# A four-layer graph network kernel: sums merged into the convolutions, a reordered setup, split loads, and a head pass with stacked columns

## Chip, cores and metric

One core of a Trainium2 chip runs the whole kernel. The metric is device time in microseconds (us) of one execution, as the median of several. An engine is one of PE (TensorE), DVE (VectorE), ACT (ScalarE), POOL (GpSimd) and SP (SyncE, which here only issues DMAs).

## What is computed

`x` has 10000 rows of 768 values. Four graph layers follow each other, each ending in a layer norm of `x + layer(x)`. The edge list has 2500 random edges and one loop for each row.

```python
edge_index = jnp.stack([src, dst])
x = _layernorm(x + _L0_gnn_ref(x, edge_index, ...))      # 2 attention convolutions, then [x, out2] @ Wu + bu
x = _layernorm(x + _L1_gnn_ref(x, W_fc, attn_l, attn_r, W_res, src, dst))   # 12 heads of 64
x = _layernorm(x + _L2_gnn_ref(x, edge_index, W, b))     # one graph convolution
x = _layernorm(x + _L3_gnn_ref(x, W1, b1, W2, b2, edge_index))              # two graph convolutions

# a head of L1:            relu(h @ W_res.T + sum over its edges e of alpha_e * (h[src_e] @ W_fc.T))
# a convolution (L2, L3):  h = x @ W;  out = segment_sum(h[src] * dinv[src] * dinv[dst], dst) + b
```

## The kernel before, in words

The 10000 rows are cut into NT = 79 tiles of 128 rows (the last has 16). Every pass goes over the 79 tiles with `over_tiles`: four tiles written out, then a hardware loop of four tiles a turn, then the rest. Each engine has its own program, and semaphores order them. UNROLL = 4 is also the number of row buffers of a pass. KC = 6 is the number of 128-wide slices of 768. In time the kernel is a row of blocks; at the end of each every engine waits for the others and the block's semaphores are cleared.

- `first_layers` (0 to 1280 us). A setup folds the norm's factor and the two attention vectors into the first weight: PE transposes W1 (L1217), makes the bias columns `c_col` with 48 one-column products (L1223), and then `fold(s)` for six slices (L1236). ACT and DVE take the folded slices out (L1115, L1109, L682, L671). ACT's queue issues the small loads first, among them 16 one-column loads of the attention vectors (L1100). `fold_const` on PE (L1246, L1250) makes a constant row from `c_col`; on PE it stands after the transposes of tile 0 and before those of tile 1, on DVE after the low part of tile 0 (L712). Then come 158 tiles of products (L1279).
- `update_pass` (1284 to 1595 us). A tile loads a row block of `out2` (L1474, into `o2`) and of `u` (L1477, into `ut`), both on one semaphore for each slot; PE turns `o2` (L1575), ACT copies it, PE multiplies (L1585), DVE adds `ut` (L1489) and takes the statistics, ACT takes the root (L1533) and normalises (L1541). `y` has two buffers. POOL clears `rows_x` (15860 columns, L1461) for the next block, and after it the padding of `o2` (L1462, L1464), for which PE waits.
- `third_layer` (1596 to 1745 us) makes the attention sums of the edges.
- `heads_pass` (1749 to 2097 us). SP loads two 64x64 weights, each twice into the diagonal blocks of a 128x128 tile (L2204, transposed element by element), then the rows (L2211). POOL fetches the summed row of the edges by an indirect DMA (L2226) and scales the own row by head (`hds_x`, L2235), DVE adds the fetched row (L2264). PE turns six slices of the row (L2355) and six of `hds_x` (L2358), ACT copies all twelve (L2312), and PE makes six pairs of 128-column products (L2368, L2369). DVE adds and takes the statistics, ACT normalises.
- Three times: `multi_sum`, a block of some 40 us, and `conv_pass`, a block of some 560 us. `multi_sum` loads and splits the next weights, fetches S2 = 6 chunks of 128 rows with indirect DMAs (L2066) into `rows`, which DVE has cleared (L2097), sums them by destination on PE (L2143, L2149), and stores the sums with indirect DMAs (L2070). `conv_pass` clears `more` on POOL (L2431), fetches one row for each row of the tile (L2440), builds `x` (L2512, L2452), turns it (L2570), splits it into a high and a low part (L2518, L2460) and makes 36 products a tile (L2581).

Of the kernel before, what the change touches and what calls it, by code (L numbers as in the profile page):

```python
# [5 lines left out]
F32 = mybir.dt.float32  # L6
# [6 lines left out]
P = 128  # L13
N = 10000
# [75 lines left out]
def over_tiles(eng, step, drain=0):  # L90


    for t in range(UNROLL):
        step(t, t, 0)
    with eng.Fori(1, NT // UNROLL) as i:
        for j in range(UNROLL):
            step(i * UNROLL + j, j, i)
    for t in range(NT // UNROLL * UNROLL, NT + drain):
        step(t, t % UNROLL, t // UNROLL)


def back(t, slot, turn, lag):

    return t - lag, (slot - lag) % UNROLL, turn + (slot - lag) // UNROLL
# [31 lines left out]
def build(nc, a, out):  # L136
# [15 lines left out]
    with ExitStack() as ctx:  # L152
# [32 lines left out]
        multi_sum(nc, g, "l2", x2, a["L2_gnn_W"], a["L2_gnn_b"])  # L185
        conv_pass(nc, g, "cv", x2, x3[0:N, :], res=x2)
        multi_sum(nc, g, "l3a", x3, a["L3_gnn_W1"], a["L3_gnn_b1"])
        conv_pass(nc, g, "c3a", x3, x2[0:N, :])
        multi_sum(nc, g, "l3b", x2, a["L3_gnn_W2"], a["L3_gnn_b2"])
        conv_pass(nc, g, "c3b", x2, out, res=x3, last=True)  # L190


# [22 lines left out]
def first_layers(nc, g, a, packed, packed2, sources, agg, h1, sc1, h2, out2, u, x2, x3):  # L215
# [3 lines left out]
    with ExitStack() as ctx:  # L219
# [85 lines left out]
        b_col, g_col, b1_col, c_col = sb("b_col", [P, KC]), sb("g_col", [P, KC]), sb("b1_col", [96, 8]), sb("c_col", [96, 8])  # L305
        b2_col, w_fc, att_t = sb("b2_col", [P, 2]), sb("w_fc", [64, 64]), sb("att_t", [64, 2, 12])
# [16 lines left out]
        att1_in = sem("att1_in")  # L323
# [48 lines left out]
        def _(sp):  # L372
# [259 lines left out]
        def _(dve):  # L632
# [569 lines left out]
        def _(pe):  # L1202
# [37 lines left out]
            def fold_const():  # L1240

                pe.wait_ge(bias_read, 1)
                pe.wait_ge(ranks, 1)
# [188 lines left out]
def update_pass(nc, g, u, out2, x1, sc3):  # L1432


    with ExitStack() as ctx:
# [15 lines left out]
        loaded = [sem(f"loaded{j}") for j in range(UNROLL)]  # L1451
# [8 lines left out]
        def _(pool):  # L1460
            nc.gpsimd.memset(g["rows_x"][:, :, :], 0.0).then_inc(rows_cleared, 1)  # L1461
            nc.gpsimd.memset(o2[:, :, 192:256], 0.0).then_inc(padded, 1)  # L1462
            pool.wait_ge(padded, 1)
            nc.gpsimd.memset(o2[:, :, 192:193], 1.0).then_inc(padded, 1)  # L1464

        @block.sync
        def _(sp):
            def step(t, slot, turn):
# [5 lines left out]
                sp.dma_start(o2[0:n, slot, 0:192], tile_rows(out2, t)).then_inc(loaded[slot], 16)  # L1474
                if at_least(t, UNROLL):
                    sp.wait_ge(prod_read, t - UNROLL + 1)
                sp.dma_start(ut[0:n, slot, :], tile_rows(u, t)).then_inc(loaded[slot], 16)  # L1477
# [1136 lines left out]
```

## Time and profile before

| | us |
|---|---|
| median of 3 runs (3906.96 to 3912.1) | 3910.45 |
| the profiled execution | 3912.32 |
| its span, first to last instruction | 3910.6 |
| PE busy | 3561.8 (91%) |
| DVE busy | 2468.7 (63%) |
| ACT busy | 1368.4 (35%) |
| POOL busy | 1119.1 (29%) |
| mean granted TensorE clock | 0.960 of 2.4 GHz |

A row of the timeline has the start, the duration, the engine with the line of the kernel, the operation, output and inputs, shapes and count, and in brackets how long the engine was idle before it and who released it. Engine names with a q (SPq, ACTq) are the queues that issue DMAs. PEld is the weight load of a matmul. An fp32 matmul leaves two records; an fp32 transpose and an fp32r matmul leave one.

### The profile page before, as it was taken

Reading aid. Unit: us, or ns where it says so; the run is one execution under the profiler, and the core shown is the slowest. Engines: PE = TensorE matmul, PEld = TensorE weight load, DVE = VectorE, ACT = ScalarE, POOL = GpSimd, SP = SyncE. Lnnn points to the kernel's source line nnn. Section 1 sums busy time; section 2 is a strip of 40 time slices with the busy share of each in tenths; the row PEclk is TensorE's granted clock in tenths of the full one; section 3 lists DMA queues with packets and bytes.
Section 4 is the critical chain, followed back from the end, with each engine's and each line's share of the span. In section 5 each row is a group of like instructions: output and inputs, shape, how many; then the busy total and the mean of one; then the engine's idle time right before and its main releaser. Section 6 shows DMA issues by size and latency. Waiting matters only on the chain. (4 is left out here: it accounts for less than half of the span.)

```text
span 3910.6 us, 64813 instructions
## 1 busy us (share of the span) xinstructions
PE 3561.8 (91%) x21189; PEld 3366.4 (86%) x21189; DVE 2468.7 (63%) x4956; ACT 1368.4 (35%) x1888; POOL 1119.1 (29%) x1536
## 2 busy tenths in 40 slices
PE   7999999999999788259996999997899998799999
PEld 7999999999999444139995999996899997799999
DVE  4877986158333588347995777775344443577777
ACT  2222232222222344115664344443333332344443
POOL 6530200315512100427884122221222221222221
PEclk8999999999999999679997999998999999899999
DMA  4777997658654688425664333333333333455554
GB/s 113 240 228 213 236 254 241 185 181 271 220 185 139 183 252 254 138 74 182 222 218 153 110 127 128 127 126 113 128 126 125 126 129 112 141 183 184 186 185 142
DMA packets 363506, 672.39 MB, mean 172 GB/s; under 512 B 100309, under 2 KB 193138, under 8 KB 363370
## 3 DMA queue, kind: packets, MB, share of 16 engines
q1 hardware_dynamic: 246490, 441.00, 37.5%
q10 hardware_dynamic: 71952, 155.79, 10.3%
q0 software_dynamic: 44928, 73.84, 6.8%
q8 instruction: 78, 1.28, 0.1%
q14 instruction: 58, 0.48, 0.0%
HBM read 429.79 MB, written 346.94 MB: 199 GB/s over the span
## 5 line engine op out<-in xcount | busy, mean ns | idle before, releaser
L712 DVE TENSOR_TENSOR fr_lo<-fr_turned_ps,fr_hi 128x768 fp32r<-128x768 f32 x158 | 150.5, 953 | 240.9 <-ACT fr_hi L1140 231.8
L2470 DVE SCALAR_TENSOR_TENSOR c3a_y<-c3a_prod,dinv,next_const 128x768 f32<-128x768 f32 x79 | 80.4, 1018 | 290.4 <-PE c3a_prod L2581 290.4
L1279 PE MATMUL fr_prod<-fr_w_hi,fr_hi 128*128 128x396 f32 x948 | 256.4, 352 | 0.0
L1279 PE MATMUL fr_prod<-fr_wu_hi,fr_hi 128*128 128x396 f32 x948 | 255.4, 350 | 0.0
L2581 PE MATMUL c3b_prod<-next_w_hi,c3b_hi 128*128 128x384 f32 x948 | 249.8, 345 | 0.0
L2581 PE MATMUL cv_prod<-next_w_hi,cv_hi 128*128 128x384 f32 x948 | 249.7, 345 | 0.0
L2581 PE MATMUL c3a_prod<-next_w_hi,c3a_hi 128*128 128x384 f32 x948 | 249.4, 344 | 0.0
L1279 PE MATMUL fr_prod<-fr_wu_lo,fr_hi 128*128 128x396 f32 x948 | 249.0, 344 | 0.0
L1279 PE MATMUL fr_prod<-fr_w_lo,fr_hi 128*128 128x396 f32 x948 | 248.9, 344 | 0.0
L1279 PE MATMUL fr_prod<-fr_w_hi,fr_lo 128*128 128x396 f32 x948 | 248.5, 343 | 0.0
L1279 PE MATMUL fr_prod<-fr_wu_hi,fr_lo 128*128 128x396 f32 x948 | 248.2, 343 | 0.0
L2581 PE MATMUL c3b_prod<-next_w_hi,c3b_lo 128*128 128x384 f32 x948 | 242.6, 337 | 0.0
L2581 PE MATMUL cv_prod<-next_w_hi,cv_lo 128*128 128x384 f32 x948 | 242.6, 337 | 0.0
L2581 PE MATMUL c3a_prod<-next_w_hi,c3a_lo 128*128 128x384 f32 x948 | 242.3, 337 | 0.0
L2581 PE MATMUL c3b_prod<-next_w_lo,c3b_hi 128*128 128x384 f32 x948 | 242.3, 337 | 0.0
L2581 PE MATMUL cv_prod<-next_w_lo,cv_hi 128*128 128x384 f32 x948 | 242.2, 337 | 0.0
L2581 PE MATMUL c3a_prod<-next_w_lo,c3a_hi 128*128 128x384 f32 x948 | 242.1, 337 | 0.0
L1140 ACT ACTIVATE fr_hi<-fr_turned_ps 128x768 fp32r<-128x768 f32 x158 | 127.3, 805 | 323.3 <-PE fr_turned_ps L1263 302.1
L1585 PE MATMUL up_prod<-w_up,up_ot 128*128 128x396 f32 x632 | 224.5, 498 | 0.9 <-DVE up_y L1489 0.7
L2518 ACT ACTIVATE c3a_hi<-c3a_turned_ps 128x768 fp32r<-128x768 f32 x79 | 64.3, 814 | 355.7 <-PE c3a_turned_ps L2570 355.7
L2368 PE MATMUL hds_prod<-hds_w_st,hds_hi 128*128 128x128 f32 x948 | 184.2, 276 | 0.0
L2369 PE MATMUL hds_prod<-hds_w_st,hds_hi 128*128 128x128 f32 x948 | 184.0, 276 | 0.0
(592 smaller groups left out, 9070.4 us busy)
## 6 DMA issues: line engine op xcount, KB each, us to landing
fr_ins<-in_x_dram SPq DMA_DIRECT2D x156, 384.0 KB
x<-fr_zrow SPq DMA_DIRECT2D x156, 384.0 KB
x<-up_x_o ACTq DMA_DIRECT2D x78, 396.5 KB
h<-fr_outs SPq DMA_DIRECT2D x78, 396.0 KB
u<-fr_outs SPq DMA_DIRECT2D x78, 396.0 KB
up_ut<-u SPq DMA_DIRECT2D x78, 396.0 KB
agg<-fr_zrow SPq DMA_DIRECT2D x78, 390.0 KB
hds_row<-x SPq DMA_DIRECT2D x78, 384.0 KB
```

The costliest lines, as they stand in the source:

```text
L712: v.tensor_tensor(lo[:, s2, :, :], turned_ps[:, 0:KC, :], hi[:, s2, :, :].bitcast(F32), ALU.subtract).then_inc(split_done, 1)
L1140: nc.scalar.activation(hi[:, t % 2, :, :], turned_ps[:, 0:KC, :], ACT.Copy).then_inc(hi_done, 1)
L1279: made = nc.tensor.matmul(prods[s2][:, bank, 0:c1 - c0], l[:, s2, s, :], w[:, s, c0:c1], start=(s == 0 and i == 0), stop=(s == KC - 1 and ...
L1585: made = nc.tensor.matmul(prods[s2][:, half, 0:HALFC], ot[:, s2, k, :], g["w_up"][:, k, half * HALFC:(half + 1) * HALFC], start=(k == 0), ...
L2368: nc.tensor.matmul(o, hi[:, s2, s, :], w_st[:, 0, :], start=True, stop=False)
L2369: made = nc.tensor.matmul(o, hi[:, s2, KC + s, :], w_st[:, 1, :], start=False, stop=True)
L2470: v.scalar_tensor_tensor(y3, p3, g["dinv"][:, bass.ds(t, 1)], c3, ALU.mult, ALU.add).then_inc(prod_read, 1)
L2518: nc.scalar.activation(hi[:, slot % 2, :, :], turned_ps[:, 0:KC, :], ACT.Copy).then_inc(hi_done, 1)
L2581: made = nc.tensor.matmul(prods[s2][:, a, 0:HALF], l[:, s2, s, :], w[:, s, a * HALF:(a + 1) * HALF], start=(s == 0 and i == 0), stop=(s == ...
```

## The change

Five parts.

1. **Setup.** The bias row is made as two 384-column products of one row for each slice, within the loop of the transposes, and turned into columns later, in `fold_const`, by eight transposes; DVE copies them out (`col_ps`, `col_read`). The 16 one-column loads on ACT's queue become 8 two-column loads on SP's, after the loads of W1 and before those of `x`.
2. **Update pass.** Separate semaphores for `o2` and `ut`: PE waits for `o2` alone, DVE for `ut`. POOL clears the padding of `o2` first and `rows_x` after it.
3. **Heads pass.** The two 64x64 weights stand one above the other in a 128x64 tile, so one product of 64 columns does what a pair of 128 columns did for half as many heads: 12 products of 64 columns in place of 12 of 128. `x` holds for each head 64 scaled and 64 own columns; ACT copies the own ones there (`beside`). All twelve transposes wait for `copied` and `built`. Eight row buffers (WIDE) in place of four. The tile loops go over eight.
4. **Sums and convolutions.** `multi_sum` and `conv_pass` are one block, `conv_layer`. `rows` and `more` live across the three, and DVE clears both in the first alone. Row loads are issued right behind the weights.
5. The degree's factor `dinv` is multiplied in by `tensor_scalar` in place of `tensor_tensor` (128x1).

```diff
# first_layers
+            with nc.allow_non_contiguous_dma(reason="small transposed loads"):
+                for k, name in enumerate(("L0_gnn_a_src1", "L0_gnn_a_dst1")):
+                    for h in range(4):
+                        sp.dma_start(w2x[:, 2 * h:2 * h + 2, 196 + k], a[name][h, :].rearrange("(q p) -> p q", p=96)).then_inc(att1_in, 16)
...
-                link(v.tensor_copy(c_col[:, :], pa[0:96, 400:408]))
-                v.memset(scrap[:, :], 0.0).then_inc(bias_read, 1)
+                v.tensor_copy(c_row.rearrange("p (a f) -> p a f", a=2), prods[1][0:1, :, 0:HALF]).then_inc(bias_read, 1)
...
             def fold_const():
+                dve.wait_ge(col_ps, 1)
+                v.tensor_copy(c_col[:, :], pa[0:96, 400:408]).then_inc(col_read, 1)
                 dve.wait_ge(const_ps, 1)
...
-                for k, name in enumerate(("L0_gnn_a_src1", "L0_gnn_a_dst1")):
-                    for q in range(8):
-                        act.dma_start(w2x[:, q, 196 + k:197 + k], a[name][q // 2, 96 * (q % 2):96 * (q % 2) + 96].rearrange("(p o) -> p o", o=1)
-                                      ).then_inc(att1_in, 16)
...
-            pe.wait_ge(small_in, 48)
-            for q in range(8):
-                for s in range(KC):
-                    made = nc.tensor.matmul(pa[0:96, 400 + q:401 + q], w1[:, s, 96 * q:96 * q + 96], b_col[:, s:s + 1],
+                if s == 0:
+                    pe.wait_ge(small_in, 48)
+                for half in range(2):
+                    made = nc.tensor.matmul(prods[1][0:1, half, 0:HALF], b_col[:, s:s + 1], w1[:, s, half * HALF:(half + 1) * HALF],
                                             start=(s == 0), stop=(s == KC - 1), skip_group_check=True)
             made.then_inc(bias_ps, 1)
...
             def fold(s):
+                if s == 1:
+                    pe.wait_ge(bias_read, 1)
...
             def fold_const():
                 pe.wait_ge(bias_read, 1)
-                pe.wait_ge(ranks, 1)
+                for q in range(8):
+                    made = nc.tensor.transpose(pa[0:96, 400 + q:401 + q], c_row[:, 96 * q:96 * q + 96], ident[0:1, 0:1])
+                made.then_inc(col_ps, 1)
+                pe.wait_ge(col_read, 1)
...
# update_pass
-            nc.gpsimd.memset(g["rows_x"][:, :, :], 0.0).then_inc(rows_cleared, 1)
             nc.gpsimd.memset(o2[:, :, 192:256], 0.0).then_inc(padded, 1)
             pool.wait_ge(padded, 1)
             nc.gpsimd.memset(o2[:, :, 192:193], 1.0).then_inc(padded, 1)
+            nc.gpsimd.memset(g["rows_x"][:, :, :], 0.0).then_inc(rows_cleared, 1)
...
+                dve.wait_ge(u_in[slot], turn * 16 + 16)
                 dve.wait_ge(multiplied, t + 1)
...
-                pe.wait_ge(loaded[slot], turn * 32 + 32)
+                pe.wait_ge(o2_in[slot], turn * 16 + 16)
...
# heads_pass
-                    for q in range(2):
-                        sp.dma_start(w_st[64 * q:64 * q + 64, k, 64 * q:64 * q + 64], w.rearrange("e d -> d e")).then_inc(w_in, 16)
+                    sp.dma_start(w_st[64 * k:64 * k + 64, :], w.rearrange("e d -> d e")).then_inc(w_in, 16)
...
-                if at_least(t, UNROLL):
-                    sp.wait_ge(prod_read, t - UNROLL + 1)
+                if at_least(t, WIDE):
+                    sp.wait_ge(prod_read, t - WIDE + 1)
...
+            def beside(t, slot, turn):
+                act.wait_ge(loaded[slot], turn * 16 + 16)
+                if at_least(t, 2):
+                    act.wait_ge(turned, t - 1)
+                nc.scalar.activation(x[:, slot % 2, :, 1, :], row[:, slot, :].rearrange("p (h f) -> p h f", h=H), ACT.Copy).then_inc(copied, 1)
...
             def step(t, slot, turn):
+                b = back(t, slot, turn, -1, WIDE)
+                if live(b[0]):
+                    beside(*b)
                 if live(t):
                     high(t, slot, turn)
...
-                pe.wait_ge(loaded[slot], turn * 16 + 16)
-                for s in range(KC):
-                    nc.tensor.transpose(turned_ps[:, KC + s, :], row[:, slot, s * P:(s + 1) * P], g["ident"][:, :])
+                pe.wait_ge(copied, t + 1)
                 pe.wait_ge(built, t + 1)
-                for s in range(KC):
-                    made = nc.tensor.transpose(turned_ps[:, s, :], x[:, slot % 2, s * P:(s + 1) * P], g["ident"][:, :])
+                for s in range(H):
+                    made = nc.tensor.transpose(turned_ps[:, s, :], x[:, slot % 2, s, :, :].rearrange("p k f -> p (k f)"), g["ident"][:, :])
...
-                for s in range(KC):
-                    o = prods[s2][:, s // 3, (s % 3) * P:(s % 3 + 1) * P]
-                    nc.tensor.matmul(o, hi[:, s2, s, :], w_st[:, 0, :], start=True, stop=False)
-                    made = nc.tensor.matmul(o, hi[:, s2, KC + s, :], w_st[:, 1, :], start=False, stop=True)
+                for s in range(H):
+                    made = nc.tensor.matmul(prods[s2][:, s // 6, (s % 6) * 64:(s % 6) * 64 + 64], hi[:, s2, s, :], w_st[:, :], start=True, stop=True)
...
# conv_layer: the engines' programs of multi_sum stand ahead of those of conv_pass in one block
+            for s in range(KC):
+                sp.dma_start(w_st[:, s, :], weights[s * P:(s + 1) * P, :]).then_inc(w_in[s], 16)
+            sp.dma_start(g["w_const"][:, :], bias.partition_broadcast(P)).then_inc(c_in, 16)
...
-            nc.gpsimd.memset(more[:, :, :], 0.0).then_inc(cleared, 1)
-            pool.wait_ge(cleared, 1)
+            if first:
+                pool.wait_ge(cleared, 2)
+            for c in range(S2):
+                source(g["src2_i"][:, c:c + 1], rows[:, c, :], arrived[c])
+            for c in range(S2):
+                pool.wait_ge(kept, c + 1)
+                put_sum(g["put2_i"][:, c:c + 1], c, put)
+            pool.wait_ge(put, 16 * S2)
...
+            if first:
+                v.memset(rows[:, :, :], 0.0).then_inc(cleared, 1)
+                v.memset(more[:, :, :], 0.0).then_inc(cleared, 1)
...
-                    v.tensor_tensor(rstd[:, s2, :], rstd[:, s2, :], g["dinv"][:, bass.ds(t, 1)], ALU.mult).then_inc(shifted, 1)
+                    v.tensor_scalar(rstd[:, s2, :], rstd[:, s2, :], g["dinv"][:, bass.ds(t, 1)], None, ALU.mult).then_inc(shifted, 1)
```

## Rows read from the trace of the kernel before

**Rows 1.** By tile, products of four passes: ns min/median/max, first and last start.
```profile
L2368 PE MATMUL hds_prod<-hds_w_st,hds_hi x948: 275/275/422, 1772.4 to 2088.4; 128*128 128x128 f32 x190
L2581 PE MATMUL cv_prod<-next_w_hi,cv_hi x948: 336/336/668, 2146.3 to 2692.9; 128*128 128x384 f32 x190
L2581 PE MATMUL c3a_prod<-next_w_hi,c3a_hi x948: 336/336/668, 2751.8 to 3297.8; 128*128 128x384 f32 x190
L2581 PE MATMUL c3b_prod<-next_w_hi,c3b_hi x948: 336/336/668, 3354.4 to 3901.1; 128*128 128x384 f32 x190
```

**Rows 2.** Timeline of the setup, 0 to 68 us.
```profile
2.82 1.09 ACTq L1097 DMA_DIRECT2D fr_b_col<-in_L_gnn_b_dram  x1
...
29.19 10.65 PE L1223 MATMUL fr_pa<-fr_b_col,fr_w 128*96 128x1 f32 x96
...
39.70 18.86 PE L1236 MATMUL fr_prod<-fr_w2x,fr_w1t 96*128 96x198 f32 x96
...
45.24 0.83 ACT L1115 ACTIVATE fr_w_st<-fr_prod 128x792 f32<-128x792 f32 x1 [11.77 <-PE fr_prod L1236]
...
61.05 2.81 PE L1250 MATMUL fr_pa<-fr_w2x,fr_b_col 96*128 96x196 f32 x16
...
65.40 0.96 DVE L712 TENSOR_TENSOR fr_lo<-fr_turned_ps,fr_hi 128x768 fp32r<-128x768 f32 x1 [1.79 <-ACT fr_hi L1140]
...
67.10 0.61 PE L1279 MATMUL fr_prod<-fr_w_hi,fr_hi 128*128 128x396 f32 x2
```

**Rows 3.** DMA issues of the first 100 us: the load of b1, last of `small_in`.
```profile
fr_b_col<-in_L_gnn_b_dram ACTq DMA_DIRECT2D x1, 3.0 KB, 18.0
```

**Rows 4.** By window: busy us (records) of each engine, granted clock, DMA share, GB/s.
```profile
34.00:36.00 2.00, 2.00 (x18) 2.00 (x18) 0.00 (x0) 0.00 (x0) 1.39 (x3) 0.64 0.06 1
```

**Rows 5.** Timeline of the update pass's start.
```profile
1283.99 13.31 POOL L1461 MEMSET rows_x<- 128x15860 f32 x1 [23.36 <-POOLq L71]
...
1297.77 1.11 PE L1575 MATMUL up_turned_ps<-ident,up_o 128*128 128x128 f32 x4 [18.46 <-POOL up_o L1464]
```

**Rows 6.** Timeline of a steady tile of the update pass.
```profile
1448.82 0.98 DVE L1489 TENSOR_TENSOR up_y<-up_prod,up_ut 128x792 f32<-128x792 f32 x1 [0.20 <-ACT up_x_o L1541]
...
1451.33 1.01 ACT L1541 ACTIVATE up_x_o<-up_y,up_shift,up_rstd 128x768 f32<-128x768 f32 x1
...
1452.45 0.98 DVE L1489 TENSOR_TENSOR up_y<-up_prod,up_ut 128x792 f32<-128x792 f32 x1 [0.20 <-ACT up_x_o L1541]
```

**Rows 7.** Timeline of the heads pass's start.
```profile
1752.74 5.23 SPq L2204 DMA_DIRECT2D hds_w_st<-in_L_gnn_W_res_dram  x2
...
1764.14 1.47 POOL L2235 TENSOR_TENSOR hds_x<-hds_row,hds_own_w 128x768 f32<-128x768 f32 x1 [7.42 <-DMA hds_row<-x]
```

**Rows 8.** By window (columns as in Rows 4: PE, PEld, DVE, ACT, POOL): 25 steady tiles of heads.
```profile
1900.00:2000.00 100.00, 100.00 (x905) 99.98 (x904) 91.03 (x251) 67.00 (x76) 88.70 (x101) 1.00 0.68 219
```

**Rows 9.** Timeline: eight fp32 products of 64 columns on other weights.
```profile
373.70 1.99 PE L1338 MATMUL fr_pa<-fr_w_fc,fr_att_t 64*128 64x64 f32 x16
```

**Rows 10.** Timeline between the first convolution and the second.
```profile
2703.50 3.90 DVE L2097 MEMSET l3as_rows<- 128x4608 f32 x1 [5.22 <-issue]
...
2708.24 0.99 POOL L2066 DMA_INDIRECT l3as_rows<-x,src_i  x1 [54.49 <-DVE l3as_rows L2097]
...
2731.86 0.98 POOL L2070 DMA_INDIRECT x<-l3as_sums,put_i  x1 [1.60 <-ACT l3as_sums L2120]
2736.59 2.66 POOL L2431 MEMSET c3a_more<- 128x3072 f32 x1 [3.75 <-POOLq L71]
...
2740.37 1.08 POOL L2440 DMA_INDIRECT c3a_more<-x,c3a_ix  x1 [0.60 <-issue]
...
2745.12 1.02 DVE L2452 SCALAR_TENSOR_TENSOR c3a_x<-c3a_more,has_in,c3a_x 128x768 f32<-128x768 f32 x1 [12.28 <-DMA c3a_more<-x,c3a_ix]
```

**Rows 11.** Timeline ahead of the third convolution.
```profile
3341.20 1.08 POOL L2440 DMA_INDIRECT c3b_more<-x,c3b_ix  x1 [0.61 <-issue]
...
3347.74 1.02 DVE L2452 SCALAR_TENSOR_TENSOR c3b_x<-c3b_more,has_in,c3b_x 128x768 f32<-128x768 f32 x1 [14.10 <-DMA c3b_more<-x,c3b_ix]
```

More of the change, by code:

```diff
@@ L87, in at_least, with over_tiles, back @@
     return not isinstance(t, int) or t >= k
-def over_tiles(eng, step, drain=0):
-    for t in range(UNROLL):
+def over_tiles(eng, step, drain=0, unroll=UNROLL):
+    for t in range(unroll):
         step(t, t, 0)
[L95 to L104, printed above, removed]
+    with eng.Fori(1, NT // unroll) as i:
+        for j in range(unroll):
+            step(i * unroll + j, j, i)
+    for t in range(NT // unroll * unroll, NT + drain):
+        step(t, t % unroll, t // unroll)
+def back(t, slot, turn, lag, unroll=UNROLL):
+    return t - lag, (slot - lag) % unroll, turn + (slot - lag) // unroll
 def live(t):
@@ L184, in build @@
         g["w_const"] = sb("next_const", [P, D])
[L185 to L190, printed above, removed]
+        g["more"], g["rows"] = sb("more", [P, UNROLL, D]), sb("rows", [P, S2, D])
+        conv_layer(nc, g, "cv", x2, x3[0:N, :], a["L2_gnn_W"], a["L2_gnn_b"], res=x2, first=True)
+        conv_layer(nc, g, "c3a", x3, x2[0:N, :], a["L3_gnn_W1"], a["L3_gnn_b1"])
+        conv_layer(nc, g, "c3b", x2, out, a["L3_gnn_W2"], a["L3_gnn_b2"], res=x3, last=True)
 class Steps:
@@ L1449, in update_pass @@
         HALFC = CU // 2
-        loaded = [sem(f"loaded{j}") for j in range(UNROLL)]
+        o2_in = [sem(f"o2_in{j}") for j in range(UNROLL)]
+        u_in = [sem(f"u_in{j}") for j in range(UNROLL)]
         stored = [sem(f"stored{j}") for j in range(UNROLL)]
@@ L2263, in add @@
                 dve.wait_ge(scaled, t + 1)
[L2264 to L2265 removed]
+                v.scalar_tensor_tensor(x[:, s2, :, 0, :], more[:, slot % UNROLL, 0:F].rearrange("p (h f) -> p h f", h=H),
+                                       g["has_in"][:, bass.ds(t, 1)], x[:, s2, :, 0, :], ALU.mult, ALU.add).then_inc(built, 1)
             def end(t, slot, turn):
@@ L2374, in step, with conv_layer @@
                     turn_over(t, slot, turn)
-                b = back(t, slot, turn, 1)
+                b = back(t, slot, turn, 1, WIDE)
                 if at_least(t, 1) and live(b[0]):
                     multiply(*b)
-            over_tiles(pe, step, 1)
-def conv_pass(nc, g, tag, table, out, res=None, last=False):
+            over_tiles(pe, step, 1, WIDE)
+def conv_layer(nc, g, tag, table, out, weights, bias, res=None, first=False, last=False):
     with ExitStack() as ctx:
@@ L2394, in conv_pass @@
         res_in = sb("res", [P, UNROLL, D]) if apart else rows_in
-        more = sb("more", [P, UNROLL, D])
+        more, rows = g["more"], g["rows"]
+        scrap_s = sb("scrap_s", [P, 3])
+        sel, car = sb("sel", [P, S2, P]), sb("car", [P, S2, P])
+        sums = sb("sums", [P, S2, D])
+        ix2 = sb("ix2", [P, 2, 2], I32)
+        w_st = sb("w_st", [P, KC, D])
         ix = sb("ix", [P, UNROLL], I32)
@@ L2507, in _, with keep, round_, rest @@
         def _(act):
+            def keep(j, b, done):
+                nc.scalar.activation(sums[:, j, :].rearrange("p (a f) -> p a f", a=2), prods[b][:, :, 0:HALF], ACT.Copy).then_inc(done, 1)
+            def round_(s):
+                act.wait_ge(w_in[s], 16)
+                nc.scalar.activation(g["w_hi"][:, s, :], w_st[:, s, :], ACT.Copy).then_inc(w_rounded, 1)
+            for c in range(S2):
+                act.wait_ge(added, c + 1)
+                keep(c, c % 2, kept)
+                if c < KC - 1:
+                    round_(c)
+            for s in range(min(S2, KC - 1), KC):
+                round_(s)
+            def rest(r):
+                for j in range(2):
+                    act.wait_ge(r_added, r * 2 + (j + 1))
+                    keep((S2 - 2) + j, j, r_kept)
+            rest_pairs(act, rest)
             def scale(t, slot, turn):
@@ L2564, in _, with add_up, rest @@
         def _(pe):
+            def add_up(slot, b, s, before, kept_by, done):
+                for a in range(2):
+                    made = nc.tensor.matmul(prods[b][:, a, 0:HALF], sel[:, s, :], rows[:, slot, a * HALF:(a + 1) * HALF],
+                                            start=True, stop=before is None)
+                if before is not None:
+                    if kept_by is not None:
+                        pe.wait_ge(*kept_by)
+                    for a in range(2):
+                        made = nc.tensor.matmul(prods[b][:, a, 0:HALF], car[:, s, :], sums[:, before, a * HALF:(a + 1) * HALF],
+                                                start=False, stop=True)
+                made.then_inc(done, 1)
+            for c in range(S2):
+                pe.wait_ge(arrived[c], 16)
+                pe.wait_ge(ready, 2 * c + 2)
+                if c >= 2:
+                    pe.wait_ge(kept, c - 1)
+                add_up(c, c % 2, c, c - 1 if c else None, (kept, c), added)
+            def rest(r):
+                pe.wait_ge(r_in, r * 32 + 32)
+                for j in range(2):
+                    pe.wait_ge(r_ready, r * 4 + (2 * j + 2))
+                    add_up(j, j, j, (S2 - 1) if j == 0 else S2 - 2, (r_kept, r * 2 + 1) if j else None, r_added)
+            rest_pairs(pe, rest)
+            pe.wait_ge(w_split, KC)
             def turn_over(t, slot, turn):
```

243 lines of the change are left out of this document (83 added, 160 removed).

## The prediction

> **What bounds the kernel now.** First the page: PE is busy 91% of the span, so time can only go where PE waits, or where its own instructions get fewer or cheaper. Then the products by tile: they give the stages and the holes between them. The last products of heads start at 2088.4 and the first of the first convolution at 2146.3; from 2692.9 to 2751.8 and from 3297.8 to 3354.4 the same. That is 57.9 + 58.9 + 56.6 = 173.4 us without products of a pass [rows 1]. Inside the three convolutions 78 tiles take 546 us, 7.0 us each, all of it PE, and nothing there is changed but one 128x1 operation on DVE, which PE doesn't wait for. The first 158 tiles are the same code too. So the change acts in five places: the setup (to 67.1 us), the start of the update pass, its steady tiles, the heads pass, and the three holes.
>
> **Setup.** Now: 48 one-column products take PE from 29.2 to 39.8 [rows 2], and they lower the clock: it is 0.64 of 2.4 GHz on average between 34 and 36 us, though PE is never idle [rows 4]. The first fold therefore ends only at 45.2, 5.5 us after its start, where 16 records cost 2.7 us at full clock (16 records of 196 columns took 2.81) [rows 2]. After: 24 records of 384 columns, each some 384/196 x 0.17 = 0.33 us, so 7.9 us, within the loop of the transposes. They can't start before `small_in` is full. Its last load is issued at 2.8 and lands 18.0 us later, at 20.8 [rows 2, 3]. From there: five slices of transposes at 8 x 0.11 = 0.9 us, 7.9 for the products, and about 2 because the clock is low at first: 35.2, against 39.8, a gain of 4.6. If the small loads land sooner, since 16 loads leave ACT's queue, it is up to 9; the eight loads on SP's queue stand before those of `x`, which are not needed until the folds are well under way. The clock is then high for the first fold: 2.8 more. Sum: 7.4 us gained up to the end of the folds.
>
> Against that stands `fold_const`. Its 40 product records (5 us, of which the 16 of L1250 are shown) now run while ACT and DVE prepare tile 0; they start at about 60.4 and end before the low part of tile 0 does, 65.40 + 0.96 = 66.4, and the first product of tile 0 comes at 67.10 [rows 2]. After the change they need `c_col`, and DVE copies it only behind that low part. So the order becomes low part, copy (0.3), constant products (5.0), transposes of tile 1 (0.8), first product: 6.4 us behind the low part in place of 0.7, a loss of 5.7. PE also waits some 6 us for the copy, after which its clock may be at the lower level: 0 to 5 more, I take 1. Net: -7.4 + 5.7 + 1 = -0.7 us; bounds -6 and +6.
>
> **Update pass, start.** PE waits for the padding of `o2`, which stands on POOL behind a memset of 13.31 us [rows 5]. With the order turned, PE waits for the first `o2` instead, issued at 1284.0. The trace shows no landing of it; from below it is about 2 us, from above the 4.75 us that a load four times as large took beside other traffic [rows 10]. I take 3, so PE starts at 1287.0 and not at 1297.8: -10.8 (-12 to -9). What is late next are the products, as before. The memset now runs beside DVE's first tiles; nobody waits for it before the next block; at most 1 us.
>
> **Update pass, steady.** PE's releaser there is mostly the load of `ut`, so splitting the semaphores looks like a gain. But the period is set elsewhere: DVE's add starts at 1448.82; its statistics release ACT's root; behind that ACT normalises the tile before, at 1451.33 for 1.01; and the next add, which needs that buffer of `y`, starts at 1452.45, 0.1 after [rows 6]. This ring of 3.63 us has neither PE nor a DMA in it. 78 x 3.63 is the pass. Gain: 0.
>
> **Heads, start.** The rows stand on SP behind four transposed loads, which it is done with at 1758.0, and the first scaling starts at 1764.1 [rows 7]. With two of them the rows go out about 5.3 us sooner (the second pair starts at 1752.7, the time at which the rows would). Against it: all twelve transposes of tile 0 now stand behind `built`, six of them more at the lower clock, 6 x 0.22 = 1.3, and a little for tile 1. Net -3.5 (-6 to -1).
>
> **Heads, steady.** 905 PE records in 100 us are 0.1105 us each, and 36 of them are a tile of 3.98 us: PE is full, DVE 91%, POOL 89%, ACT 67% [rows 8]. The change leaves the count at 36 and halves the columns of 24. What is a record of 64 columns worth? Elsewhere in this kernel 16 of them took 1.99 us, less 0.27 for the last one's tail [rows 1, 9]: 1.72/15 = 0.115 us, no less than one of 128. So the weight load sets the pace and halving the columns brings nothing: a tile is 12 x 0.1105 + 24 x (0.1105 to 0.115) = 3.98 to 4.09. I take +0.025 a tile, +2 us (0 to +8).
> The Trainium skill ("TensorE: Matmul & The Clock Gate", LDWEIGHTS) says the same from the weight's side: a load takes its columns divided by 1.2 GHz, 107 ns for 128, whatever streams. Its formula for the gap of a lone matmul in the same part (columns divided by 2.4 GHz, plus 2.5 ns) speaks the other way and would make two fp32 passes of 64 columns about half as dear, PE's tile 2.7 us. The row decides for the first; the second is a rival.
> The new copy on ACT (128x768, nearest row 1.01 us [rows 6]) makes ACT 67 + 25 = 92% busy; it hides beside PE as long as a tile is over 3.7 us. The eight buffers take away waits of POOL for rows, which cost nothing while PE is full. The six own-row transposes were PE's cover (0.66 us) for a late `built`; that cover is gone. DVE's tile of 3.64 us busy leaves 0.3, which I take as enough.
>
> **The three holes.** In the second [rows 10]: (a) the clearing of `rows` (3.90) no longer stands ahead of the first fetch: 2708.24 - 2703.50, -4.7. (b) the clearing of `more` on POOL, -2.7. (c) between the end of the last store's issue (2732.84) and POOL's next work (2736.59) lie 3.75 us: the store's landing and the reading of a count, which stay, and the block's end, which goes: 0 to 3.75, I take -1.5. (d) the first fetch takes 2745.12 - 2740.37 = 4.75 us beside the row loads of that block, which now are long done; alone I take 3.4 (between its issue of 1.1 and this): -1.3. Sum -10.2. In the third, (d) is 6.54 us, since twice as many rows are loaded [rows 11]: -3.1, sum -12.0. In the first, DVE clears `more` too before the first fetch, 3072/4608 x 3.90 = 2.6 later, so only (c) and a small (d) are left: -1.8. In all three the row loads now run beside the fetches of the sums, 1.6 MB (3.1 in the third) on top of 4.7 MB. The sums are a chain between PE and ACT of 2.6 us a chunk, slower than the fetches arrive, so I give this +0.5 each. Total -22.5 (-31 to -11).
>
> **Sum.** -0.7 - 10.8 + 0 - 3.5 + 2 - 22.5 = -35.5 us. Against the profiled execution 3912.3 - 35.5 = 3876.8; it lay 1.9 above the median of the runs, so against that 3910.45 - 35.5, 3875 us.
>
> **Rivals.**
> 1. *Narrow products are cheap* (0.12). PE's tile falls to 2.7 and DVE sets it at about 3.85 (3.64 busy and its waits): 79 x -0.15 = -12, another -2 for the term above: 3861. Against it: rows 9.
> 2. *The fetches of the sums stand behind the row loads* (0.13). Then the first chunk arrives when some 4.3 MB are in, about 11 us at an estimated 385 GB/s, and (a) brings nothing in the second and third hole: +10 to +13: 3887.
> 3. *The lost cover shows* (0.13). `built` or `copied` comes late and the tile of heads becomes 4.2: 79 x 0.2 = +16: 3891. For it: DVE at 91% [rows 8].
> 4. *The split loads do help* (0.06). If the ring were only apparent, the update tile would fall to DVE's own 3.4: 78 x -0.23 = -18: 3857.
> 5. *Slower than before: the clock falls in the heads pass* (0.04). One-column products lowered it with PE never idle [rows 4]; 64-column ones stream half of what the pass streams now. At 1.2 GHz every record doubles, as the first fold did: 4 us more a tile, up to +316. From 9 of 79 tiles on (35.5/4) the whole gain is gone. With half the tiles it is 4033. Against it: the transposes stay, and the records still stream more than half the time. The Trainium skill ("TensorE: Matmul & The Clock Gate", Part 4) holds that transposes don't count as activity, which would make this likelier; in the setup here the clock has risen during transposes alone.
>
> **How the numbers follow.** Forecast 0.52, at 3875, own range 3862 to 3886. The range of 8 in 10 takes in cases 1, 2 and 4 and half of 3: 3855 to 3892. A measurement of this kernel tells about 0.2%, 8 us, from no change. Faster by over that: all but case 5 and a pile-up of cases 2 and 3 with a bad setup, 0.92; within it 0.03; slower 0.05.
>
> **What would show it.** Setup: no stretch of low clock before the first fold, but one before the constant's products, and the first product of tile 0 near 66. Update: PE from 1287 less the shift, period still 3.63. Heads: 36 records a tile at 0.11, period 4.0 to 4.05, ACT near 90%. Holes: 47 to 49 us for the second, 45 to 47 for the third, 56 for the first. Wrong it would be through a heads tile other than 4.0, or first fetches that land over 6 us after their issue.

## The result, and the profile after

The changed kernel is slower: 3934.9 us (median of four runs, 3932.5 to 3935.3) against 3910.8 (3907.0 to 3912.1), a ratio of 1.0058 with an interval of 1.0045 to 1.007. Forecast were 3875 and a range of 3855 to 3892 for 8 cases in 10. The profiled execution has a span of 3930.4 us against 3910.6, so the balance below adds up to +19.8.

First the products by tile again, as in [rows 1] (ns min/median/max, first and last start), with those of the first block and of the update pass.

```profile
L1284 PE MATMUL fr_prod<-fr_w_hi,fr_hi x948: 337/343/677, 67.5 to 664.7; 128*128 128x396 f32 x190
L1284 PE MATMUL fr_prod<-fr_wu_hi,fr_hi x948: 339/343/677, 666.2 to 1271.9; 128*128 128x396 f32 x190
L1592 PE MATMUL up_prod<-w_up,up_ot x632: 496/496/868, 1282.0 to 1570.0; 128*128 128x396 f32 x158
L2238 PE MATMUL hds_prod<-hds_w_st,hds_hi x1896: 222/275/422, 1753.5 to 2134.8; 128*128 128x64 f32 x190
L2569 PE MATMUL cv_prod<-next_w_hi,cv_hi x948: 336/336/668, 2191.5 to 2735.9; 128*128 128x384 f32 x190
L2569 PE MATMUL c3a_prod<-next_w_hi,c3a_hi x948: 335/336/668, 2786.0 to 3330.2; 128*128 128x384 f32 x190
L2569 PE MATMUL c3b_prod<-next_w_hi,c3b_hi x948: 336/336/668, 3376.6 to 3920.8; 128*128 128x384 f32 x190
```

The two rows of before that [rows 1] leaves out:

```profile
L1279 PE MATMUL fr_prod<-fr_wu_hi,fr_hi x948: 339/343/667, 672.3 to 1278.2; 128*128 128x396 f32 x190
L1585 PE MATMUL up_prod<-w_up,up_ot x632: 496/496/1027, 1298.9 to 1583.9; 128*128 128x396 f32 x158
```

From differences of these starts:

| stretch | before | after | change | forecast |
|---|---|---|---|---|
| start to first product | 67.1 | 67.5 | +0.4 | -0.7 |
| 158 tiles | 1211.1 | 1204.4 | -6.7 | 0 |
| to the first product of update | 20.7 | 10.1 | -10.6 | -10.8 |
| update | 285.0 | 288.0 | +3.0 | 0 |
| to the first product of heads | 188.5 | 183.5 | -5.0 | -3.5 |
| heads | 316.0 | 381.3 | **+65.3** | +2 |
| three holes | 173.4 | 153.2 | -20.2 | -22.5 |
| three convolutions | 1639.3 | 1632.8 | -6.5 | 0 |
| end | 9.5 | 9.6 | +0.1 | 0 |

Everything outside heads brought 45.5 us, somewhat more than the 37.5 forecast; 13 of it, in the 158 tiles and the convolutions, were not forecast and are not explained (see below). Heads went from 4.05 to 4.89 us a tile and took it all back. The same 100 us as in [rows 8] (busy us and records of PE, weight loads, DVE, ACT, POOL, then clock, DMA share, GB/s):

```profile
1900.00:2000.00 100.00, 86.62 (x733) 84.67 (x733) 93.88 (x205) 68.32 (x81) 58.16 (x81) 0.97 0.52 176
```

PE is no longer full (87%) and POOL has more time to spare than before, but DVE is at 94%: 4.6 us a tile in place of 3.64, though the change gave it only 0.05 us more work (the factor, 0.21 in place of 0.16). One tile says where that microsecond is (timeline, rows of DVE and POOL alone):

```profile
1901.57 1.02 DVE L2126 SCALAR_TENSOR_TENSOR hds_x<-hds_more,has_in,hds_x 128x768 f32<-128x768 f32 x1 [0.41 <-issue]
...
1902.50 0.22 DVE L2120 SCALAR_TENSOR_TENSOR hds_own_w<-hds_more,has_in,has_own 128x12 f32<-128x12 f32 x1
1902.64 0.15 DVE L2146 RECIPROCAL hds_rstd<-hds_root 128x1 f32<-128x1 f32 x1
...
1902.86 1.47 POOL L2097 TENSOR_TENSOR hds_x<-hds_row,hds_own_w 128x768 f32<-128x768 f32 x1 [1.81 <-DVE hds_x L2126]
1902.94 0.22 DVE L2148 TENSOR_SCALAR hds_rstd<-hds_rstd,dinv 128x1 f32<-128x1 f32 x1
1903.19 1.16 DVE L2150 SCALAR_TENSOR_TENSOR hds_shift<-hds_mv,hds_rstd 128x1 f32<-128x1 f32 x1
...
1904.27 0.95 DVE L2134 SCALAR_TENSOR_TENSOR hds_y<-hds_prod,hds_row 128x768 f32<-128x768 f32 x1
```

The shift, one element a lane, takes 1.16 us. It ends at 1904.35, and POOL's multiply ends at 1904.33. Over the pass (by tile):

```profile
L2150 DVE SCALAR_TENSOR_TENSOR hds_shift<-hds_mv,hds_rstd x79: 159/1176/1271, 1761.6 to 2139.1; 128x1 f32<-128x1 f32 x79
```

Before, its median was 159 ns, and in a steady tile the multiply started 1.2 us behind it (timeline of before):

```profile
1902.64 0.16 DVE L2288 SCALAR_TENSOR_TENSOR hds_shift<-hds_mv,hds_rstd 128x1 f32<-128x1 f32 x1
...
1903.84 1.47 POOL L2235 TENSOR_TENSOR hds_x<-hds_row,hds_own_w 128x768 f32<-128x768 f32 x1 [0.47 <-DMA hds_row<-x]
```

The reason to be tested, **theory S**: a DVE operation with two inputs in SBUF doesn't run while POOL's multiply, which reads SBUF, does. Before, the load of the row ended POOL's wait ahead of 28 of the 79 multiplies; in the changed kernel it does so once. Now POOL stands ready, `own_w` releases it, and DVE issues `own_w` just ahead of its three small operations. (The profile puts 45 of the waits down to DVE's add, the operation just ahead of `own_w`, and 15 to `own_w`; by the program the multiply waits for `own_w`.) The Trainium skill ("SBUF — State Buffer", Who interferes with whom) states this as a lock on a pair of ports that VectorE and GpSimd share, which two SBUF inputs on DVE need against a GpSimd instruction that reads SBUF. The rows above agree. **Rival P**: with all twelve transposes behind the build, the tile is longer by itself. **Rival F**: the scalar operand of the degree's factor sets it off.

### The profile page after: what moved, and what is told of

Same layout as the page of the kernel before. It is cut to its first block and busy times, and to the rows that moved or that the text cites. A ratio compares the mean times of both kernels' runs of the same rounds, so it can differ in the third digit from the quotient of the medians.

```text
span 3930.4 us, 64494 instructions
## 1 busy us (share of the span) xinstructions
PE 3575.6 (91%) x21125; PEld 3371.2 (86%) x21125; DVE 2542.9 (65%) x4955; ACT 1425.3 (36%) x1967; POOL 1058.3 (27%) x1532
## 3 DMA queue, kind: packets, MB, share of 16 engines
q10 hardware_dynamic: 70160, 155.79, 10.2%
## 5 line engine op out<-in xcount | busy, mean ns | idle before, releaser
L1140 ACT ACTIVATE fr_hi<-fr_turned_ps 128x768 fp32r<-128x768 f32 x158 | 127.3, 806 | 326.7 <-PE fr_turned_ps L1268 326.6
L2238 PE MATMUL hds_prod<-hds_w_st,hds_hi 128*128 128x64 f32 x1896 | 223.9, 275 | 0.0
L1592 PEld LDWEIGHTS up_prod<-w_up,up_ot 128*128 128x128 f32 x632 | 114.7, 191 | 125.8 <-ACT up_ot L1535 45.4
L2238 PEld LDWEIGHTS hds_prod<-hds_w_st,hds_hi 128*128 128x128 f32 x1896 | 222.3, 195 | 0.0
```

Source lines behind the costliest of these rows:

```text
L1140: nc.scalar.activation(hi[:, t % 2, :, :], turned_ps[:, 0:KC, :], ACT.Copy).then_inc(hi_done, 1)
L1592: made = nc.tensor.matmul(prods[s2][:, half, 0:HALFC], ot[:, s2, k, :], g["w_up"][:, k, half * HALFC:(half + 1) * HALFC], start=(k == 0), ...
L2238: made = nc.tensor.matmul(prods[s2][:, s // 6, (s % 6) * 64:(s % 6) * 64 + 64], hi[:, s2, s, :], w_st[:, :], start=True, stop=True)
```

## Experiments in the heads pass

A run that is given without an interval was executed once, so a few us of its time can be chance; there the trace counts more than the time.

**heads_before.** The changed kernel with the pass of before.

> The changed kernel with the heads pass of before; everything else is the changed one. All theories: the whole loss sits in that pass (78 tiles took 381 us of products against 316), so this must come out near 3911 - 45 = 3866 us, about 1.8% under the changed kernel; over 3880 would mean that part of the loss is elsewhere.

Measured: 3882.4 us, 0.9900 of before on that chip (3917.8; 0.9883 to 0.9918). Products of heads 319.2 us. By the ratio it is 1.6% under the changed kernel, some 62 us (1.8% expected): the loss is in the pass. The time lies over the 3880 of the expectation, on a chip on which before is 7 us slower. In this profile the 158 tiles took 1213.1 us, 8.7 more than in that of the changed kernel, in code that is the same in both.

**four_rows.**

```
-    H, F, WIDE = 12, D, 2 * UNROLL
+    H, F, WIDE = 12, D, UNROLL
```

> The changed kernel with four row buffers in heads in place of eight, nothing else. Theory S: a DVE operation with two inputs in SBUF (the shift, 128x1) can't run while POOL's multiply (1.47 us) does; eight row buffers took away the wait for rows that had kept POOL's multiply late, so it now starts 0.1 to 0.4 us behind own_w and ahead of the shift. With four buffers the wait is back: shift 0.16 us, tile 4.0 to 4.1 us, 3934.9 - 60 = 3868 to 3876 us. Rival P (all twelve transposes behind the build, which is ACT's copy and DVE's add, lengthen the tile whatever the rows do): the tile stays at 4.8 to 4.9 and the time at 3935. Rival F (the scalar operand of the factor): stays at 3935 too.

Measured: 3879.8 us (before 3917.8 on that chip); 326.7 us for 78 tiles, 4.19 each. The shift is back at 0.16, and what holds the multiply back is seen: ACT's copy waits 0.5 to 0.6 us for the row, and POOL's multiply starts beside it, 0.46 us behind the shift's start (timeline of four_rows):

```profile
1902.09 0.16 DVE L2150 SCALAR_TENSOR_TENSOR hds_shift<-hds_mv,hds_rstd 128x1 f32<-128x1 f32 x1
1902.18 0.96 DVE L2134 SCALAR_TENSOR_TENSOR hds_y<-hds_prod,hds_row 128x768 f32<-128x768 f32 x1
1902.42 0.84 ACT L2175 ACTIVATE hds_x<-hds_row 128x768 f32<-128x768 f32 x1 [0.50 <-DMA hds_row<-x]
1902.55 1.47 POOL L2097 TENSOR_TENSOR hds_x<-hds_row,hds_own_w 128x768 f32<-128x768 f32 x1
```

Fewer buffers, 55 us less in the pass, with the twelve transposes and the scalar operand as they were: against P and F. The tile was forecast at 4.0 to 4.1 and the time at 3868 to 3876. PE is busy 98% here; POOL waits for rows ahead of 32 multiplies, and DVE's add for the multiply in 15 tiles, which is the likely reason for 4.19.

**factor_tt.**

```
-v.tensor_scalar(rstd[:, s2, :], rstd[:, s2, :], g["dinv"][:, bass.ds(t, 1)], None, ALU.mult)
+v.tensor_tensor(rstd[:, s2, :], rstd[:, s2, :], g["dinv"][:, bass.ds(t, 1)], ALU.mult)
```

> The changed kernel with the degree's factor in heads as a TENSOR_TENSOR of two SBUF inputs again, nothing else. Theory S: the wait moves one operation forward, the factor takes some 1.2 us and the shift 0.16; tile 4.9, time 3935 within 6. Rival F (the scalar operand sets it off): factor and shift 0.16 each, tile 4.0 to 4.1, 3865 to 3875. Rival P: nothing moves at all, the shift stays at 1.2.

Measured: 3951.1 us (before 3917.8), tile 5.06, more than the 4.9 expected. As S said, the wait moved to the operation that now has two SBUF inputs and comes first (by tile):

```profile
L2150 DVE SCALAR_TENSOR_TENSOR hds_shift<-hds_mv,hds_rstd x79: 159/160/1326, 1767.5 to 2157.6; 128x1 f32<-128x1 f32 x79
L2148 DVE TENSOR_TENSOR hds_rstd<-hds_rstd,dinv x79: 159/1426/1658, 1765.8 to 2157.4; 128x1 f32<-128x1 f32 x79
```

F falls, it points the other way: the scalar operand had saved 0.17 us a tile (4.89 against 5.06). With the scalar operand the factor runs beside the multiply, and the shift ends as the multiply does; here the factor ends as the multiply does, and the shift's 0.16 us come behind.

**order_swap.** In DVE's step (calls shortened):

```
+shift_of(t - 3)
 own(t + 1)
-shift_of(t - 3)
 end(t - 2)
```

> The changed kernel with DVE's steps of heads in another order: reciprocal, factor and shift ahead of own_w, which releases POOL's multiply; the same instructions. Theory S: the multiply then starts behind the shift and runs beside the sum from PSUM and the statistics, which have one SBUF input; shift 0.16 us, DVE's tile 3.7 us busy, tile set by PE's 36 records at 4.0, at most 4.2; 3934.9 - 65 = 3870 (3862 to 3885). Rival P: the tile stays at or over 4.7. Rival F: as P, the scalar operand is still there.

Measured: 3873.3 us, 0.9881 (0.9863 to 0.9898); tile 4.12, shift at most 0.162 us in all 79. The same instructions in another order are worth 1.8%. P falls with it. (PE is busy 98.5% here, 885 records in 100 us; why not fully is not shown.)

**shift_ts.**

```
-v.scalar_tensor_tensor(shift[:, s2, :], mv[:, s2, 0:1], -1.0, rstd[:, s2, :], ALU.mult, ALU.mult)
+v.tensor_scalar(shift[:, s2, :], mv[:, s2, 0:1], rstd[:, s2, :], -1.0, ALU.mult, ALU.mult)
```

> The changed kernel with heads' shift as a TENSOR_SCALAR: the mean from SBUF, the factor and -1 as scalar operands, so one SBUF input in place of two; order and buffers as in the changed kernel. Theory S (two SBUF inputs on DVE can't run beside POOL's multiply): the shift takes 0.21 us although the multiply runs, tile 4.0 to 4.1, about 0.988 of before as with the other order. Rival (any small DVE operation behind own_w is caught by the multiply): shift still 1.2, tile 4.9, 1.006 of before.

Measured: 3866.4 us, 0.9881 (0.9861 to 0.9902), before 3914.2. The timeline of a tile:

```profile
1902.34 0.15 DVE L2146 RECIPROCAL hds_rstd<-hds_root 128x1 f32<-128x1 f32 x1
1902.56 1.47 POOL L2097 TENSOR_TENSOR hds_x<-hds_row,hds_own_w 128x768 f32<-128x768 f32 x1 [0.44 <-DVE hds_x L2126]
1902.63 0.21 DVE L2148 TENSOR_SCALAR hds_rstd<-hds_rstd,dinv 128x1 f32<-128x1 f32 x1
...
1902.88 0.21 DVE L2150 TENSOR_SCALAR hds_shift<-hds_mv,hds_rstd 128x1 f32<-128x1 f32 x1
1903.01 0.95 DVE L2134 SCALAR_TENSOR_TENSOR hds_y<-hds_prod,hds_row 128x768 f32<-128x768 f32 x1
```

The multiply runs, and neither small operation waits: it isn't their place but their second SBUF input. Nor is it the kind of operation: `hds_y` is a SCALAR_TENSOR_TENSOR as the shift was, with one of its inputs in PSUM, and doesn't wait either. The window shows PE full again, so the pass is back at its old bound, 311.5 us for 78 tiles, 3.99 each:

```profile
1900.00:2000.00 100.00, 100.00 (x911) 99.81 (x910) 92.49 (x253) 82.76 (x101) 72.03 (x103) 1.00 0.70 220
```

911 records are 0.1098 us each, two thirds of them 64 columns wide. So the narrow products brought nothing, as forecast, and the clock stayed at 1.00. The tile is 0.13 us shorter than in order_swap, but the two ratios don't tell them apart.

**before_wide.** Does the number of buffers do it alone? The kernel of before, with `row` and `loaded` eight deep; the tile loops of this pass go over eight too, as in the changed kernel (not shown).

```
-    H, F = 12, D
+    H, F, WIDE = 12, D, 2 * UNROLL
...
-        row, more = sb("row", [P, UNROLL, D]), sb("more", [P, UNROLL, AGG_W])
+        row, more = sb("row", [P, WIDE, D]), sb("more", [P, UNROLL, AGG_W])
...
-                if at_least(t, UNROLL):
-                    sp.wait_ge(prod_read, t - UNROLL + 1)
+                if at_least(t, WIDE):
+                    sp.wait_ge(prod_read, t - WIDE + 1)
```

> The kernel of before with eight row buffers in heads, nothing else (its products of 128 columns, six transposes of the row ahead of the build, no copy on ACT). Theory S in its strong form (the wait for rows alone kept the multiply late): factor or shift over 1 us, tile 4.8 to 5.0, before + 60 to 80 us. Weak form (the rows are one of two things; POOL's small operation behind DVE's add, 0.9 us instead of 0.19, also holds it back, and PE's transposes of the row fill its time): tile stays at 4.0 to 4.1, before + 0 to 8.

Measured: 4000.6 us, before 3914.2: +86, of which the pass is 79. Products 395.3 us, 5.07 a tile. The strong form holds, a little over its range (timeline of DVE and POOL, one tile):

```profile
1951.09 0.23 DVE L2258 SCALAR_TENSOR_TENSOR hds_own_w<-hds_more,has_in,has_own 128x12 f32<-128x12 f32 x1
...
1951.46 1.47 POOL L2235 TENSOR_TENSOR hds_x<-hds_row,hds_own_w 128x768 f32<-128x768 f32 x1 [1.61 <-DVE hds_x L2264]
1951.62 1.32 DVE L2286 TENSOR_TENSOR hds_rstd<-hds_rstd,dinv 128x1 f32<-128x1 f32 x1 [0.23 <-DVE hds_rstd L2284]
```

The load of the row ended POOL's wait once in 79 tiles, in place of 28 times. This is the cause: four buffers had kept two engines out of each other's way, by a wait of POOL that cost nothing. No run separates the eight buffers from the tile loops over eight. That the row's load no longer ends POOL's waits speaks for the buffers, and shift_ts, which has the loops over eight, takes 3.99 us a tile.

## Experiments outside heads

**clear_again.** `if first` around the two memsets and the wait for them became `if True`.

> The changed kernel with the clearing of the two row tiles (DVE, 3.9 and 2.6 us) ahead of the fetches of the sums in all three convolutions, not in the first alone. The step of the forecast by which this clearing stood on the path: the second and third hole grow from 50.1 and 46.4 us by 6.5 each, 13 in all, the first stays at 56.7; time 3934.9 + 13 on a chip as fast as the first. Rival (the fetches wait for the row loads or weights anyway): they grow by under 2 each.

Measured: 3956.4 us (before 3914.2). The first hole is 56.6 as in the changed kernel, the second 57.0 (+6.9), the third 55.4 (+9.0). From the last product to POOL's first fetch it is 18.6 and 15.1 us in place of 10.5 and 6.9, some 8.1 each: the memsets (3.90 and 2.62), 0.6 between them and 0.8 behind. The clearing stood on the path: 15.9 us in the two holes, 13 expected.

**swap_const, ts_const, reload_late.** In the changed setup PE waits for DVE's copy of the bias column, then runs the first 20 of the constant's 32 product records at the lower clock; the granted clock is 0.50 from 58 to 60 us, 0.53 from 60 to 65 and 1.00 from 65 to 67 (timeline of PE, changed kernel):

```profile
58.45 1.69 PE L1251 MATMUL fr_pa<-fr_w2x,fr_c_col 96*128 96x198 f32 x4 [5.42 <-DVE fr_c_col L690]
...
59.93 5.19 PE L1255 MATMUL fr_pa<-fr_w2x,fr_b_col 96*128 96x196 f32 x16
```

The 16 records took 5.19 us in place of the 2.81 of [rows 2]. The edit moves the eight 1x1 transposes behind the second fold and DVE's copy behind the first two low parts, out of `fold_const` (the lines that go there are not shown):

```
             for s in range(KC):
                 fold(s)
+                if s == 1:
+                    for q in range(8):
+                        made = nc.tensor.transpose(pa[0:96, 400 + q:401 + q], c_row[:, 96 * q:96 * q + 96], ident[0:1, 0:1])
+                    made.then_inc(col_ps, 1)
...
                     fold_low(s)
+                    if s == 1:
+                        dve.wait_ge(col_ps, 1)
+                        v.tensor_copy(c_col[:, :], pa[0:96, 400:408]).then_inc(col_read, 1)
```

> The kernel with DVE's other order in heads, and in the setup the eight 1x1 transposes of the bias row behind the second fold and DVE's copy of them behind the first two low parts, so that the constant's 40 products follow the transposes of tile 0 without a wait. By my reading of the setup the products now wait 5.4 us for DVE's copy, behind the low part of tile 0, and then run at the lower clock; without it they take 5 us beside the low part, and the first product of tile 0 comes at 59 to 60 in place of 66.3 to 67.5: 7 to 8 us less than the kernel with the other order alone, 0.986 of before. If another thing holds tile 0, the gain is under 3 us.

Measured: 3869.8 us, 0.9887 (0.9871 to 0.9904) against 0.9881 for the order alone, though the first product came at 59.4 in place of 66.3. The expectation failed: 7 us were gained at the start, 2.8 of them were left at the end of the 158 tiles (1274.5 against 1277.3), and none shows in the time. In the trace PE waits 8.3 us near 275, against 3.3 in order_swap. I formed **theory Q**: SP waits for POOL's last scatter ahead of tile 29, and the loads of `x` stand behind that wait. With the TENSOR_SCALAR shift in place of the order:

> The kernel with heads' shift as a TENSOR_SCALAR and with the constant's products of the setup freed of their wait (transposes of the bias row behind the second fold). Theory Q (a wait in SP's queue takes the gain back): PE reaches tile 0 some 8 us sooner, but SP waits ahead of tile 29 for the last scatter of POOL (264 to 268 us) with the loads of x behind it, so PE waits there that much longer: 0.986 to 0.988 of before, gain over the TENSOR_SCALAR kernel alone (0.9881) 0 to 3 us. If nothing takes it back: 7 to 8 us less, 0.986 or lower, and PE's wait near 275 stays at 3 us.

Measured: 3864.7 us, 0.9869 (0.9852 to 0.9885), before 3915.6. Its timeline, POOL, SP, DVE and PE:

```profile
265.21 1.19 POOL L501 DMA_INDIRECT packed<-fr_rec,fr_ix  x1 [0.30 <-issue]
267.67 0.31 SPq L440 DMA_DIRECT2D fr_sd_r<-packed  x1
...
268.79 0.36 SPq L385 DMA_DIRECT2D fr_ins<-in_x_dram  x1
272.04 0.56 DVE L702 BATCH_NORM_STATS2 fr_stats<-fr_ins 128x6 f32<-128x384 f32 x1 [15.95 <-DMA fr_ins<-in_x_dram]
277.52 1.51 PE L1266 MATMUL fr_turned_ps<-ident,fr_xn 128*128 128x128 f32 x6 [10.63 <-DVE fr_lo L717]
```

This is the whole chain: last scatter, reload, load, statistics, PE after 10.6 us. The time lies in Q's range (0.986 to 0.988). The 158 tiles end 2.8 us sooner than in shift_ts (1275.7 against 1278.5), though they start 8.9 sooner. The next kernel turns `AT_RELOAD, AT_LISTS` from 29, 31 to 30, 32.

> As the kernel before it, and SP's wait for the scatters, with the reload of their lists, one tile later (ahead of tile 30 in place of 29), DVE's use of the lists one tile later too. Theory Q: the loads of x ahead of it go out in time, PE's wait of 8 us near 275 goes down by 4 to 7, the last product of the first 158 tiles comes 3 to 7 us earlier, 0.985 to 0.987 of before. Rival: the loads are late because of the traffic after the scatters, not because of the queue; then under 1 us changes, or it moves to DVE, which waits for the lists.

Measured: 3860.9 us, 0.9862 (0.9845 to 0.9878). The intervals of the two overlap, so their times don't tell them apart; the traces do (reload_late):

```profile
264.20 1.19 POOL L501 DMA_INDIRECT packed<-fr_rec,fr_ix  x1 [0.30 <-issue]
266.68 0.31 SPq L440 DMA_DIRECT2D fr_sd_r<-packed  x1
...
276.70 1.16 PE L1266 MATMUL fr_turned_ps<-ident,fr_xn 128*128 128x128 f32 x6 [3.12 <-DVE fr_lo L717]
```

Scatter and reload come 1.0 us sooner, PE's wait falls from 10.6 to 3.1, and the last tiles of the block end 5.7 us sooner (1270.0 against 1275.7). At 1.4% under before, this has the lowest median of the study.

**old_setup.** The kernel shift_ts with the first block of before.

> The kernel with heads' shift as a TENSOR_SCALAR, but with the first block (setup and first 158 tiles) of before. Forecast: the setup is worth -0.7 us, so within 1 of the TENSOR_SCALAR kernel (0.9881 of before). Theory Q says the same for another reason, that the wait ahead of tile 29 levels differences of the setup. First product of tile 0 near 67 in both.

Measured: 3867.0 us, 0.9879 (0.9863 to 0.9896), against 0.9881. No worth of the new setup is to be seen.

**old_update.** The kernel shift_ts with the update pass of before.

> The kernel with heads' shift as a TENSOR_SCALAR, but with the update pass of before (the memset of 13.3 us ahead of the padding, one semaphore for both loads). Forecast: PE's first transposes 10.8 us later against the end of the 158 tiles (19.9 us between last and first product in place of 9.4), and the same 3.63 us a tile; the pass itself took 285.0 us from first to last product there and 288.0 in the changed kernel, which should come back too, so net +7 to +8 us.

Measured: 3877.9 us (before 3915.6). Last product to first product 20.7 us in place of 10.2, pass 286.5 in place of 288.0, net +9.0.

## Why the prediction was wrong

- **The step that failed** is in "Heads, steady": "The eight buffers take away waits of POOL for rows, which cost nothing while PE is full." The wait cost nothing; taking it away cost 65 us, since it also set when the multiply starts. I asked what POOL gains by it, and not what runs on DVE at the time to which the multiply moves. The trace of before had shown the price, in a tile at the start of the pass where the two met (timeline):

```profile
1780.88 1.47 POOL L2235 TENSOR_TENSOR hds_x<-hds_row,hds_own_w 128x768 f32<-128x768 f32 x1 [1.83 <-DMA hds_row<-x]
...
1781.30 1.07 DVE L2286 TENSOR_TENSOR hds_rstd<-hds_rstd,dinv 128x1 f32<-128x1 f32 x1
```

  1.07 us for one element, until 1782.37, with the multiply ending at 1782.35, and a wait for a row ahead of it. In steady tiles POOL's one-element operation took 0.96 us beside DVE's add, for 0.19 elsewhere: the same the other way round. I had used neither row.
- "DVE's tile of 3.64 us busy leaves 0.3, which I take as enough" assumed that durations stay when phases move. Rival 3 had the right pass and the right side, but priced a late `built` at 0.2 us a tile; it was 0.84, for another reason.
- **Right in heads:** 36 records at 0.11, narrow products no gain (3.99 a tile in shift_ts, forecast 4.0), no fall of the clock (rival 5: 1.00 in the window above), ACT's copy hidden. Without the collision the pass is 4.5 us shorter than before (311.5 against 316.0), where I had added 2.
- **Holes:** forecast -1.3, -9.7 and -11.5, measured -1.2, -8.8 and -10.2. The first fetch took 3.0 us from issue to use in the second (2776.32 to 2779.34; forecast 3.4), and rival 2 didn't come at its size. But the fetches of the sums were held up beside the row loads: from the issue of the first to PE's first product of the sums it is 6.7, 7.6 and 7.5 us in the three holes, for 6.3, 5.9 and 5.2 before, 4.4 more in all where the forecast allowed 1.5.
- **Update:** the start came out as forecast (-10.6 for -10.8), by two errors that cancel: the first `o2` was in 2.0 us after its issue (forecast 3), and PE then waited 1.3 us for the second `o2`, which I hadn't counted. The ring is as forecast, 3.63 us from add to add (1449.29 to 1452.92). The pass cost 3 us that I had put at nothing. 1.3 of them are the products of tile 0, which stay at the lower clock longer: the granted clock was 0.50 from 1279 to 1286 and 0.82 to 1288, before 0.50 and 0.52 from 1297 to 1301 and then 1.00; in both PE had been idle ahead of it. The add of tile 0 comes 5.3 us behind the first product in place of 4.0:

```profile
1282.03 5.15 PE L1592 MATMUL up_prod<-w_up,up_ot 128*128 128x396 f32 x8
```

  Before, these eight records took 3.89 us. Another 0.9 is the memset's microsecond, allowed for in the text but not in the sum: a DVE operation of 0.23 us took 1.13, until the memset's end, and the second add comes 4.26 us behind the first in place of 3.34. The rest, some 0.8, is spread over the tiles. The split of the loads brought nothing in steady tiles.
- **Setup:** the folds ended 8.0 us sooner (forecast 7.4). The constant's chain took 9.2 us behind the low part, not 6.4 and 1 for the clock, because 20 of its 32 product records (I had counted 40) ran at the lower clock: the 16 above took 2.4 us more. Sum +0.4 for -0.7. Missed was that the sum hardly matters: SP's wait levels it.
- **Not foreseen, and partly open:** the 158 tiles took 6.7 us less in the profile after. It isn't the change: seven other profiles with the same block show 1208.2 to 1213.8 us from first to last start, before shows 1211.1. In the profile after POOL's last scatter was at 257.66, elsewhere at 263.5 to 274.1. Why it was early there is open. So is the gain in the convolutions, 543.9 to 544.8 us each in every kernel with the merged blocks and 546.0 to 546.7 in the two without: a tile is 0.03 us shorter with PE full in both.

Without the collision the change would have come to 0.988 of before, some 3864 us on the first chip, inside the range; as said, in part by gains that were not forecast.

## What to carry to other kernels

A wait that costs nothing can still be what keeps two engines apart: before removing it, ask at what time the released work will now run, and what runs on the other engines then. DVE operations with two SBUF inputs shouldn't be issued between the operation that releases POOL work that reads SBUF and the end of that work; put them ahead of it, or give them scalar operands. A gain ahead of a queue's wait on another engine is only worth something up to that wait.

## What the runs showed of the hardware

A one-element DVE operation with two SBUF inputs took 1.16 to 1.43 us, to the end of POOL's 1.47 us multiply, against 0.16; with one SBUF input and scalar operands 0.21 beside the same multiply. The other way round, POOL's one-element operation with SBUF inputs took 0.9 beside DVE's add of two SBUF inputs (timeline of before) and 0.19 beside a DVE operation with its second input in PSUM (changed kernel, at 1904.54):

```profile
1901.10 1.00 DVE L2264 SCALAR_TENSOR_TENSOR hds_x<-hds_more,has_in,hds_x 128x768 f32<-128x768 f32 x1
...
1901.18 0.96 POOL L83 TENSOR_TENSOR hds_scrap_p<-ones 128x1 f32<-128x1 f32 x1
```

A pure write was different: during POOL's memset of 13.31 us a two-input DVE operation took its 0.16, and a TENSOR_SCALAR of 24 elements 1.13 in place of 0.23 (timeline of the changed kernel, memset from 1278.00 to 1291.31):

```profile
1290.14 0.16 DVE L1510 SCALAR_TENSOR_TENSOR up_shift<-up_mv,up_rstd 128x1 f32<-128x1 f32 x1
1290.22 1.13 DVE L1511 TENSOR_SCALAR up_part<-up_y,up_rstd 128x24 f32<-128x24 f32 x1
```

The Trainium skill ("SBUF — State Buffer", Who interferes with whom) has both halves of this: two inputs contend only with reads, and `tensor_scalar` may enter a mode that takes both ports. No run here separates the modes.
